# The tile loop of an attention and mixture-of-experts kernel rewritten: k in four partition groups, q by column groups, statistics by accumulated sums, another order on every engine

## The reference, cut to what matters

```python
# x: 4 images, 256 channels, 32x32 pixels; wq, wk: 32x256; wv: 256x256
q, k, v = x*wq + bq, x*wk + bk, x*wv + bv              # 1x1 convolutions
energy = einsum('bci,bcj->bij', q, k)                  # 1024x1024 per image, 32 terms
attn = softmax(energy over groups of 32 columns)
x = gamma * einsum('bchk,bhwkv->bcwv', v, attn) + x
t = tokens(x)                                          # 4096 tokens of 256
t = t + (ln(t) @ W1 + (band @ ln(t)) @ W2 + bias)      # band: weights 1..32 of the 32 tokens before
u = ln(t)
sel = sigmoid(u @ expert_sel.T); two best of 32 experts
t = t + sum over the two: sel_e * relu(u @ keys_e) @ values_e
```

## Time and profile before

| | before |
|---|---|
| median of 3 runs | 510.26 us (509.55 to 510.54) |
| profiled execution, its own time | 509.37 us |
| profiled execution, span | 507.6 us |
| PE, PEld busy | 399.3, 292.9 us |
| DVE, ACT, POOL busy | 362.7, 229.5, 321.6 us |
| granted PE clock, mean | 0.878 |
| first stage, steps 2 to 31 | from 27.95 us to about 283 us |

### The profile page before, as it was taken

How to read it: one execution, slowest core, us unless ns; L and a number is a source line. 1 busy time by engine, 2 the same in 40 slices (tenths; PEclk the granted TensorE clock), 3 DMA queues, 4 the chain that set the end, 5 groups by cost and what they waited for, 6 DMA issues and landing times.

```text
span 507.6 us, 10650 instructions
## 1 busy us (share of the span) xinstructions
PE 399.3 (79%) x3207; PEld 292.9 (58%) x3207; DVE 362.7 (71%) x1080; ACT 229.5 (45%) x604; POOL 321.6 (63%) x479
## 2 busy tenths in 40 slices
PE   8899999999999999999999885748676277766000
PEld 4677777877778877777676662336454154534000
DVE  3778999999999999999999667546454454556100
ACT  2214454544555454545454343339655556735000
POOL 5345558888778888688888777144555554636610
PEclk9899999999999999999999976879877768767555
DMA  8996001411111111121110012575554443431096
GB/s 202 330 213 182 11 23 54 126 53 44 53 33 47 49 54 44 44 52 45 54 52 35 22 63 74 134 234 156 164 153 133 124 135 109 123 95 50 3 206 125
DMA packets 28441, 49.55 MB, mean 98 GB/s; under 512 B 6204, under 2 KB 21966, under 8 KB 27373
## 3 DMA queue, kind: packets, MB, share of 16 engines
q1 hardware_dynamic: 20512, 26.69, 20.6%
q0 software_dynamic: 7872, 22.19, 14.1%
HBM read 30.74 MB, written 25.73 MB: 111 GB/s over the span
## 4 chain that ended last, share of the span: by engine, by line
PE 51%; issue 14%; DVE 13%; SPq 9%; POOL 3%; DMA 2%; another core or an unknown queue 1%; ACT 1%; DVEq 0%; POOLq 0%; ACTq 0%
PE bank L1189 17%; SPq L396 8%; PE bank L1129 6%; PE bank L1070 6%; PE E L1094 5%; PE bank L1243 3%; PE bank L1049 2%; PE E L1229 2%; PE bank L1162 2%; PE bank L1257 2%; DVE gmax L744 2%; POOL out L568 2%; PE bank L1170 2%; DVE gsum L792 2%; PE bank L1149 2%
## 5 line engine op out<-in xcount | busy, mean ns | idle before, releaser
L568 POOL DMA_INDIRECT out<-vT,dest x80 | 78.8, 985 | 68.7 <-DVE vT L1003 47.9
L1189 PE MATMUL bank<-vT,prob 128*128 128x256 f32 x512 | 118.8, 385 | 0.0
L1189 PEld LDWEIGHTS bank<-vT,prob 128*128 128x128 f32 x512 | 95.7, 191 | 12.2
L490 POOL TENSOR_TENSOR prob<-prob,ginv 128x1024 f32<-128x1024 f32 x32 | 61.0, 1907 | 28.1 <-DVE ginv L807 25.6
L472 POOL DMA_INDIRECT slot_rows<-rows,slot x64 | 68.4, 1069 | 12.7 <-issue 12.7
L990 DVE TENSOR_SCALAR q_s<-bank 128x256 f32<-128x256 f32 x20 | 8.5, 424 | 63.1 <-remote 56.1
L1257 PE MATMUL bank<-rows,q_s 64*64 64x256 f32 (+1 forms) x224 | 36.2, 479 | 19.2 <-DVE q_s L990 10.8
L665 ACT ACTIVATE prob<-E 128x512 f32<-128x512 f32 x40 | 22.7, 593 | 55.2 <-PE E L1229 34.5
L628 ACT ACTIVATE prob<-prob 128x1024 f32<-128x1024 f32 x32 | 33.8, 1057 | 20.8 <-DVE prob L748 20.8
L1243 PE MATMUL bank<-prob,k_s 128*64 128x64 f32 (+1 forms) x448 | 32.1, 297 | 13.9 <-issue 13.2
L1229 PE MATMUL E<-ident,xc_or_xin 128*128 128x128 f32 x160 | 28.9, 336 | 16.7 <-DMA xc_or_xin<-slot_rows 15.6
(11 more groups left out here) (200 smaller groups left out, 856.7 us busy)
## 6 DMA issues: line engine op xcount, KB each, us to landing
xc_or_xin<-slot_rows SPq DMA_DIRECT2D x48, 130.0 KB
xc_or_xin<-slot_rows SPq DMA_DIRECT2D x64, 65.0 KB
xt<-x_tok SPq DMA_DIRECT2D x32, 128.0 KB, 2.4
values_s<-values SPq DMA_DIRECT2D x2, 2048.0 KB, 28.3
out<-out POOLq DMA_DIRECT2D x4, 1024.0 KB, 14.1
xc_or_xin<-x_cm SPq DMA_DIRECT2D x3, 1024.0 KB, 20.3
keys_s<-keys SPq DMA_DIRECT2D x1, 2048.0 KB, 14.2
out<-vT,dest POOLq DMA_INDIRECT x80
```

The lines of the kernel that those rows point to most:

```text
L490: g.tensor_tensor(prob[:, t % 2], prob[:, t % 2], ginv[:, t % 2].unsqueeze(2).to_broadcast([P, WT * KB, W]), ALU.mult).then_inc(prob_done, 1)
L568: g.indirect_dma_start(out=out, out_offset=bass.IndirectOffsetOnAxis(ap=dest[:, n % (2 * NB), k:k + 1], axis=0), in_=yb[:, n % NB, k, :], ...
L1189: mm = m.matmul(av_p, pr[:, j, :], vT[:, b % 2, j, :], start=(j == 0), stop=(j == KB - 1))
```

## The change

- **k in four partition groups.** The weights of k stand four times beside each other, so one matmul gives k in all four groups of 32 partitions. k of the next image is made in four pieces of 256 columns in the steps 3 to 6 of an image, and ACT moves each out as one 128x256 operation.
- **q by column groups.** In step 2, eight matmuls of 128 rows and 32 columns write q into four partition groups, and one 128x256 operation of ACT moves it out.
- **Energies.** The 16 matmuls of a tile use four row groups and four column groups of the array, one matmul for each of the 16 blocks; before they used two row groups, two matmuls for each of 8 blocks. E lies in four half-filled PSUM banks, no longer in two full ones.
- **Statistics.** The two sums on DVE also give their row sums (a scalar_tensor_tensor with accum_out). The variance comes from a Square with accum_out on ACT (128x256), and one more 128x1 operation of ACT adds the epsilon. The bn_stats and bn_aggr of DVE and two small operations of POOL per tile are gone.
- **Order.** Every engine's step has a new order. Both transposes of PE now stand before the energies; v comes after mix and waits for the first sum of the same step, because both lie in one PSUM bank; DVE moves v out at the start of the next step.

The diff, cut to its core:

```diff
@@ -57,7 +57,7 @@
 S_AV, S_TURN, S_MIX, S_NORM2, S_ROUTE, S_POS, S_SEND = 1, 2, 3, 4, 5, 6, 7
 LAST = S_SEND
 RB = 5
-QK_STEPS = (5, 6)
+Q_STEP, K_STEPS = 2, (3, 4, 5, 6)
...
+                    if s < NT - 1:
+                        scatter_rows(t, 1)
                 for t in tiles(s, S_NORM2):
                     second_factors(t)
+                scale_by_sums(s)
...
-            def q_evac(b, c):
-                act.wait_ge(qk_mm, 2 * b + c + 1)
+            def q_evac(b, src):
+                act.wait_ge(q_mm, b + 1)
                 after(act, e_mm, TB * (b - 1))
-                for r in range(2):
-                    from_q, beside_k = slice(2 * r * QK, (2 * r + 1) * QK), slice((2 * r + 1) * QK, (2 * r + 2) * QK)
-                    src = qk_bank(b, c)[from_q, :].rearrange("p (t r n) -> p t r n", r=2, n=WT // 2 * H)[:, :, r, :]
-                    qa = a.activation(q_s[beside_k, b % 2, c * TB // 2:(c + 1) * TB // 2].rearrange("p t w h -> p t (w h)"),
-                                      src, ACT.Identity, bias=bqk[from_q, 0:1])
-                qa.then_inc(q_out, 1)
+                a.activation(q_s[:, b % 2].rearrange("p t h -> p (t h)"), src, ACT.Identity, bias=bqk[:, 1:2]).then_inc(q_out, 1)
+
+            def k_evac(b, u):
+                act.wait_ge(k_mm, k_made(b - 1) + u + 1)
+                after(act, e_mm, TB * (b - 1))
+                vs = W // len(K_STEPS)
+                a.activation(k_s[:, b % 2, :, :, u * vs:(u + 1) * vs], qk_p.rearrange("p (v j g) -> p g j v", g=WT, j=KB),
+                             ACT.Identity, bias=bqk[:, 0:1]).then_inc(k_out, 1)
...
+            def squared(x, mv_t, rstd_t, t, x_done, rstd_done, mv_done, ve_done):
+
+                act.wait_ge(x_done, t + 1)
+                after(act, ve_done, t)
+                a.activation(squares[:, :], x, ACT.Square, bias=mv_t[:, 0:1], scale=-float(C),
+                             accum_out=mv_t[:, 1:2]).then_inc(mv_done, 1)
+                act.wait_ge(mv_done, t + 1)
+                after(act, rstd_done, t - 1)
+                a.activation(rstd_t[:, 0:1], mv_t[:, 1:2], ACT.Identity, bias=eps_col[:, 0:1], scale=1.0 / C ** 3).then_inc(ve_done, 1)
...
+            for s in range(NT):
+                for t in tiles(s, S_MIX):
+                    turned(t)
+                for t in tiles(s, S_ROUTE):
+                    second_turned(t)
+                    logits_exp(t)
+                for t in tiles(s, S_TURN):
+                    first_norm(t)
+                for t in tiles(s, S_ROUTE):
+                    second_copy(t)
+                act.wait_ge(centred, s + 1)
+                a.activation(prob[:, s % 2], prob[:, s % 2], ACT.Exp).then_inc(exp_done, 1)
                 for t in tiles(s, S_NORM2):
...
+                work = proj_work(s)
+                if work and work[1] == Q_STEP:
+                    q_evac(work[0], qk_p)
+                elif work and work[1] in K_STEPS:
+                    k_evac(work[0], K_STEPS.index(work[1]))
+                for t in tiles(s, S_NORM2):
+                    second_norm(t)
+                for t in tiles(s, S_MIX):
+                    z_high(t)
+                for t in tiles(s, S_AV):
+                    first_squares(t)
+                for t in tiles(s, S_ROUTE):
+                    columns_written(t)
...
+                v.scalar_tensor_tensor(out=t1[:, t % 3], in0=av_p, scalar=1.0, in1=xt[:, t % 4], op0=ALU.mult, op1=ALU.add,
+                                       accum_out=mv1[:, t % 2, 0:1]).then_inc(t1_done, 1)
...
+                v.scalar_tensor_tensor(out=t2[:, t], in0=h_at(t), scalar=1.0, in1=t1b[:, t % 2], op0=ALU.mult, op1=ALU.add,
+                                       accum_out=mv2[:, t % 2, 0:1]).then_inc(t2_done, 1)
...
             for s in range(NT):
-                work = proj_work(s)
+                work = proj_work(s - 1)
+                if work:
+                    v_evac(work[0], work[1])
                 for t in tiles(s, S_NORM2):
-                    dve.wait_ge(z_hi_done, t + 1)
-                    v.tensor_tensor(z_lo[:, t % 3], z_at(t), z_hi[:, t % 3].bitcast(F32), ALU.subtract).then_inc(z_lo_done, 1)
...
+                    z_low(t)
+                dve.wait_ge(e_mm, s + 1)
+                v.tensor_reduce(gmax[:, s % 2].rearrange("p (w j) -> p w j", w=WT), E.rearrange("p w (j v) -> p w j v", v=W),
+                                AX.X, ALU.max).then_inc(max_done, 1)
+                dve.wait_ge(max_done, s + 1)
...
+                    second_sum(t)
+                for t in tiles(s, S_ROUTE):
+                    dve.wait_ge(ex_done, t + 1)
+                    v.tensor_scalar(ex1[:, t % 2], ex[:, t % 2], 1.0, None, ALU.add).then_inc(ex1_done, 1)
+                for t in tiles(s, S_MIX):
+                    turned_low(t)
...
+                dve.wait_ge(exp_done, s + 1)
+                v.tensor_reduce(gsum[:, s % 2], prob[:, s % 2], AX.X, ALU.add).then_inc(sum_done, 1)
+                for t in tiles(s, S_ROUTE):
+                    dve.wait_ge(top_done, t + 1)
+                    v.max_index(topi[:, t % 2], top[:, t % 4], sig[:, t % 2]).then_inc(topi_done, 1)
+                dve.wait_ge(sum_done, s + 1)
+                after(dve, prob_done, s - 1)
+                v.reciprocal(ginv[:, s % 2], gsum[:, s % 2]).then_inc(inv_done, 1)
...
+                for t in tiles(s, S_AV):
+                    first_sum(t)
...
+                for a in range(CH):
+                    tokens = xc[:, b % 2, a, :].rearrange("p (t w h) -> p w t h", w=WT, h=H)
+                    for c in range(WT):
+                        mm = m.matmul(dst[c * QK:(c + 1) * QK, :], wqk[:, a, 4 * QK:5 * QK], tokens[:, c],
+                                      start=(a == 0), stop=(a == CH - 1))
+                mm.then_inc(q_mm, 1)
...
+                for c in range(WT):
                     for g in range(WT):
-                        for r in range(2):
-                            at = slice((2 * r + 1) * QK, (2 * r + 2) * QK)
-                            cols = slice((r * 2 + w) * KB * W, (r * 2 + w + 1) * KB * W)
-                            mm = m.matmul(E[g * H:(g + 1) * H, cols], q_s[at, b % 2, tb, w, :],
-                                          k_s[at, b % 2, g].rearrange("p j v -> p (j v)"), start=True, stop=True)
+                        at = slice(c * QK, (c + 1) * QK)
+                        mm = m.matmul(E[g * H:(g + 1) * H, c, :], q_s[at, b % 2, tb, :],
+                                      k_s[at, b % 2, g].rearrange("p j v -> p (j v)"), start=True, stop=True)
...
+                b = t // TB
+                pe.wait_ge(prob_done, t + 1)
+                pe.wait_ge(v_out, min(t + 1 + TB, B * KB))
+                after(pe, t1_done, t)
+                pr = prob[:, t % 2].rearrange("p (j w) v -> p j (w v)", w=WT)
+                for j in range(KB):
+                    mm = m.matmul(av_p, pr[:, j, :], vT[:, b % 2, j, :], start=(j == 0), stop=(j == KB - 1))
+                mm.then_inc(av_mm, 1)
...
+            def turn(t):
+                pe.wait_ge(u1_done, t + 1)
+                after(pe, uT_lo_done, t)
+                for a in range(CH):
+                    mm = m.transpose(uT_p[:, a, :], u1[:, t % 2, a * P:(a + 1) * P], ident[:, :])
+                mm.then_inc(uT_mm, 1)
...
+            for s in range(NT):
+                for t in tiles(s, S_ROUTE):
+                    second_turn(t)
+                if s > 1:
                     energies(s)
...
+                for t in tiles(s, S_NORM2):
+                    memory(t)
+                for t in tiles(s, S_ROUTE):
+                    logits(t)
+                for t in tiles(s, S_AV):
+                    attend(t)
+                for t in tiles(s, S_POS):
+                    positions(t)
+                work = proj_work(s)
...
+                    after(pe, uT_lo_done, s - S_TURN)
+                    if j == Q_STEP:
+                        q_proj(b, qk_p)
...
+                        k_proj(b, K_STEPS.index(j))
+                for t in tiles(s, S_MIX):
+                    mix(t)
+                if work:
+
+                    after(pe, t1_done, s)
+                    if s == 0:
+                        pe.wait_ge(v_out, KB)
+                    v_proj(work[0], work[1], v_p)
+                for t in tiles(s, S_TURN):
...
+                    turn(t)
```

More of the change, by code:

```diff
@@ L1206, in _ @@
+                for t in tiles(s, S_TURN):
+                    turn(t)
+                if s == NT + 1:
                     mix(NT - 1)
-                if work and work[2]:
-                    v_proj(work[0], work[1])
-                    bank6_v[0] = v_evacs[0]
             for _ in range(PLAN_WARM):
-                m.matmul(bank[7][:, :], ones_b[:, :], warm[:, :], start=True, stop=True)
+                m.matmul(bank[7], ones_b[:, :], warm[:, :], start=True, stop=True)
             pe.wait_ge(sched_done, 4)
```

541 lines of the change are left out of this document (238 added, 303 removed).

## The result

The changed kernel takes 515.06 us (median of four runs, 513.49 to 516.97), the kernel before 509.9 us beside it (four runs, 507.79 to 510.54). The ratio on record is 1.0136, with a 95% interval of 1.0091 to 1.0182; it is an estimate of its own, and the two medians by themselves give 1.0101. On another chip the ratio was 1.0102 (1.0075 to 1.0129). So the change is a small loss. The prediction was 507.8 us, faster: the wrong sign, and the time is 0.06 us above the range of 503 to 515. The profiled execution took 515.35 us, span 513.6.

A forecast was written before the change was run, and what follows sets the result against it. PE and DVE were both taken as the bound. From 509.4 us, tile 9 comes 1.2 late, tiles 9 to 24 gain 2.3, bare steps 1.4, drain 0: -2.5; plus 0.9 for the median gives 507.8 us, range 503 to 515.

The forecast's parts named there:

- DVE's list to the first sum: DVE's instructions from the energies' maximum to the first sum, priced row by row: 6.0 us together.
- the closed way: One-step loop through PE and DVE: v, transposes, energies, maximum, first sum, v again; 8.27 us, keeping plain steps at 8.3.
- The drain: Pipeline running empty after the tile loop: one square more, one bn pair less; counted 0, with 1.5 us on both sides.
- Energies: PE's 16 matmuls per tile on 16 blocks: 0.65 us instead of 1.03, 0.38 off PE.
- Rival C: PE's energies don't shrink and take over 0.80 us; 515.4 us, slower than before; chance 0.10.
- q: PE's new q step: eight matmuls, 16 records, four column groups side by side in four rounds, 1.03 us.
- rival E: q's column groups on PE run one after the other, 2.4 us for each of four images; 517.4 us; chance 0.04.
- Accumulators: Read-outs of the row sums: 0.08 us each on DVE, 0.2 us on ACT.
- The idle time of 0.38 us before v: PE in plain steps waits 0.38 us before v for DVE's first sum, so the step keeps 8.3 us.
- rival B: PE's own sum also bounds plain steps, DVE's list to the first sum being 0.4 us shorter; 503.8 us; chance 0.20.
- PE's own sum: PE's work per step without waits: plain 7.92 us, with k 8.79, with q 8.95.
- ACT's way in bare steps: Second closed way, through PE and ACT's copies, square and accumulator: 7.77 us, so bare steps take 7.8 instead of 8.0.

The follow-up runs named there:

- e2: Changed kernel with one wait more: POOL's scale starts only when DVE has multiplied the picked slots; 470.60 us, ratio to the kernel before 1.0014.
- g1: The changed kernel itself, unchanged, run once more on another chip; 516.64 us against 511.74 for the kernel before, ratio 1.0102.
- e1: Changed kernel with two neighbours on DVE exchanged, hotb now ahead of seen; 477.8 us in one execution.
- e4: Changed kernel with z_hi of tile 29 moved ahead of the copy of turned tile 30 in ACT's drain; 475.0 us, ratio to the kernel before 1.0116.
- g2: Changed kernel with e2's wait, e4's z_hi move, uT_hi and u2T ahead of tile 30's squares, z_lo ahead of uT_lo; 502.82 us, ratio to the kernel before 0.9833.
- h1: The kernel of e2 again (changed kernel with the scale's wait alone), on another chip; 506.28 us, ratio to the kernel before 0.9976.
- h2: Changed kernel with g2's three changes of order in the drain, without the scale's wait; 510.84 us, ratio to the kernel before 1.0057.

## Why the prediction was wrong

**The step that failed** is in the part on the change, where DVE's list to the first sum was priced row by row and the work behind it not at all. The front showed that L763, L773, L779 and L784 had moved behind the first sum. The prediction took them out of the closed way and asked nothing of their new place. There POOL's scale runs, and the first that reads two SBUF tensors waits for its end: 1.6 us. The sum had one way closed through DVE and PE, and none for DVE's list by itself. That list grew to 8.50 us in plain and 8.1 in bare steps and became the bound.

What it cost: without the lock the loop is 6.2 us shorter (242.38 against 248.60). By steps, from the starts of the energies: 0.64 from tile 2 to 9, 2.79 from 9 to 24 (132.47 against 129.68), 2.79 in the bare steps (56.59 against 53.80). It is far less than 26 x 1.5 = 38 us, because in the changed kernel DVE has idle time that takes most of it up: without the lock (e2) it waits 0.41 and 0.55 us in a plain step, and longer in k steps. What was left is 0.36 us in a plain step, 0.4 in a bare and in a q step, and at most 0.24 in a k step. In the kernel before, whose DVE had no such time, the same move cost 41 us in the loop and 45 in all.

For POOL's two long operations the rows say it without exception. In all traces together seen starts 128 times and hotb 37 times while a scale has more than 0.15 us to run, and each ends 0.03 to 0.05 us after the scale; beside t1b, POOL's other long operation, hotb does so 14 times. spot, the first sum, z_lo and uT_lo read one tensor from SBUF and one from PSUM; they stand beside the scale 291 times and are never longer (spot took 0.11 us from start to start in the rows above). Nor does everything on POOL do it. Beside POOL's scatters seen, hotb, hot and picked keep their 0.2 to 0.3 us, and so does hot beside the 128x1 factors, with 0.27 us of their row still to run. The Trainium skill, "SBUF — State Buffer", section "Who interferes with whom", states such a rule: a VectorE instruction with two SBUF inputs contends with a GpSimd instruction that reads SBUF, through ports that are an exclusive lock, and whoever issues first blocks the other. The waits beside the scale and t1b agree with it, POOL being first in each; beside the 128x1 factors no wait is seen. In the drain of the changed kernel hotb took 0.75 us beside POOL's t1b of 0.72 (291.19 to 291.91):

```profile
291.21 0.75 DVE L909 TENSOR_TENSOR hotb<-hot 128x32 bf16<-128x32 f32 x1
```

```profile
291.19 0.72 POOL L480 TENSOR_TENSOR t1b<-t,biasb 128x256 f32<-128x256 f32 x1
```

**The second step** that failed is "The drain ... I count 0 with 1.5 on both sides": it took 3.8 us more in the profiled execution and 2.2 and 2.6 more in two later traces (g1, e1), against the one trace of the kernel before. It counted operations in the chain and not what stands ahead of them. In the drain PE starves, and each z_lo decides. z_lo of tile 28 came behind seen, which stood in the lock, and behind uT_lo, for which ACT had first to do the squares of tile 30; z_hi of tile 29 came behind the squares of tile 31 and the copy of a tile not yet made. PE waited 2.09 and 1.57 us for z_lo, and the rows after each wait are at half clock:

```profile
287.30:290.80 3.50, 3.50 (x14) 3.18 (x15) 1.89 (x11) 1.61 (x6) 1.16 (x3) 0.52 0.11 38
290.90:294.70 3.80, 3.80 (x19) 3.33 (x18) 0.99 (x3) 0.25 (x1) 3.03 (x4) 1.00 0.11 37
298.10:302.60 4.50, 4.47 (x16) 3.83 (x17) 2.69 (x13) 1.96 (x6) 2.46 (x5) 0.50 0.11 33
```

With both repairs the drain takes 41.34 us, 2.3 less than before the change (e2, e4, g2, h1 and h2 above). How much of this is the shorter waits and how much the clock was not taken apart.

**The rest of the sum held, in part by errors that cancel.** Without the lock (e2) tile 9 starts at 87.32 (predicted 87.8), 9 to 24 takes 129.68 (129.7), the bare steps 53.80 (54.6). Term by term:

- Energies: 0.64 to the next matmul (0.65). The trace's single records start 7 ns apart in two rounds of 16, the second 0.24 us after the first, much as the prediction read rows 2. Rival C, which wanted 0.80, is out. The Trainium skill's rule that the prediction weighed ("TensorE: Matmul & The Clock Gate", section "Wait — 56ns, not 53.3ns?"), starts never closer than about 25 ns, is not borne out here: its 0.8 us and more stand against 0.64.
- q: 1.00 us (1.03), rival E is out: below, 16 records, and mix 1.00 after.
- Accumulators: 0.08 on DVE (0.08), 0.19 and a gap of 0.03 on ACT (0.2).
- The closed way: in e2 v 85.82, energies 87.32, maximum 88.22, first sum 93.49, v 93.98, so 8.16 (8.27). The prediction's list left out MAX_INDEX (L849), which runs mostly beside the end of the sum of the exponentials: from that sum to the reciprocal the rows have 1.29 us, the prediction 1.24.
- The idle time of 0.38 us before v did not come, with the lock or without. In e2's plain step PE follows on without a bracket: its own list takes nearly all of the 8.15 us, not 7.92. That v still waits for the first sum a little can be read only from its four records, 1.13 us long there and 1.02 in the changed kernel, where v came late. So the plain step ended near the forecast with two bounds within about 0.1 us of each other, which is close to rival B and partly luck.
- PE's own sum: k 8.65 to 8.90 (8.79), q 9.14 (8.95), plain about 8.05 (7.92; 8.15 less the 0.1 of the wait above, an estimate). It was up to 0.2 short: two transposes in a row and the energies behind them cost 0.53, not the 0.41 of the rows before.
- ACT's way in bare steps: 7.71 (7.77), and PE waits for u2T there.

```profile
102.20 1.07 PE L1081 MATMUL bank<-xc_or_xin,wqk 128*32 128x256 f32 x16
103.20 0.51 PE L1160 MATMUL bank<-w_hi,uT_hi 128*128 128x512 f32 x1
```

```profile
87.06 0.50 ACT L611 ACTIVATE squares<-t,mv 128x256 f32<-128x256 f32 x1
87.46 0.19 ACT L611 ACTIVATION_READ_ACCUMULATOR squares<-t,mv 128x1 f32 x1
87.69 0.29 ACT L615 ACTIVATE rstd<-mv,eps_col 128x1 f32<-128x1 f32 x1
```

The sum of errors closes: the profiled execution was predicted at 506.9 and took 515.35. Of the 8.4 us the loop holds 277.04 - 272.1 = 4.9 (the lock's 6.2, less 1.3 by which the other terms were too dear), the drain 3.8, the second stage -0.3.

None of the named rivals came in the changed kernel. The prediction had no mechanism in which DVE becomes the bound by a longer instruction, though its list was read as full; so the 0.32 for slower rested on other reasons than the one that came.

**What stays open.** That the lock needs POOL to read SBUF, and not only to write it, was not tried. The rows settle that a long tensor operation of POOL is enough (128x1024 or 128x256) and that a scatter is not. No run was made on why the 128x1 operations don't do it, nor on what happens when DVE's instruction starts first. The repairs' gain (0.9833 against 1.0102, 13.8 us by the medians) is larger than what the two profiled executions show (514.28 and 503.52, 10.8 us: 6.0 in the start of tile 31, 4.5 in the drain, 0.3 in the second stage). The rest is the spread of the runs of the changed kernel, of which the profiled one was the fastest; no other of these runs was traced.

## What to carry to other kernels

When an instruction moves, look at what the other engines do at its new place, not only at what stands around it in its own list. Above all lay DVE's operations with two SBUF inputs beside POOL's long ones: 0.17 us of work became 1.67. A wait on the engine with slack, ahead of its long instruction, can pay: here it gave 6.2 us. What the lock costs depends on DVE's slack: 6 us in the loop of the changed kernel, 41 in that of the kernel before. And price a drain by what stands ahead of each link of the chain in the engines' lists: with PE starved such items are paid, and in this case again in the matmuls behind them, at a granted clock of 0.50 to 0.52.

## What the runs showed that was not expected

- The lock moves with the first instruction that reads two SBUF tensors, and ends within 0.05 us of POOL's.
- Energies issued twice cost 0.78 us more, where two more rounds at 0.216 would be 0.43. In the trace's single records the second pass begins with a gap (all but one record of its first round start 0.41 us or more behind the last round of the first pass, where the two rounds of one pass are 0.24 apart), and most of its starts are 17 ns apart, not 7. Why is not shown.
- The same kernel before took 470.29 us on one chip and 508.19 to 511.74 on others. The kernel before was not traced on the fast chip; the kernel of e2 was traced on both (e2 and h1), with the same tile loop to 0.1 us (242.38 and 242.41), and padr to the end of the span took 151.7 us (468.9 - 317.24) there and 187.8 (505.1 - 317.29) here.
